# Flamingo block with experts: turned context and later weights laid out by the host, gate weights as one block of 16 columns

## The reference, cut to what matters

```python
x = x + tanh(g_xattn[0]) * xattn0(layernorm(x), ctx)   # 16 heads of 128, RMS-normed q and k, softmax
x = x + tanh(g_ffn[0])   * ffn0(layernorm(x))          # W, 8 LoRA experts of rank 16, top 2 by gate_w
x = x + tanh(g_xattn[1]) * xattn1(layernorm(x), ctx)   # Q'K / sqrt, sigmoid, V; Q, K, V are x, ctx, ctx
x = x + tanh(g_ffn[1])   * ffn1(layernorm(x))          # 8 experts of rank 64, the one with the largest logit
...
# ffn1
logits = xf @ Wg.T ; gate = argmax(softmax(logits)) ; h = (xf @ A.T) * one_hot(gate) ; y = h @ Bw * 4 * prob
```

## Time and profile before

| | us |
|---|---|
| median of 3 runs | 1327.33 |
| lowest and highest run | 1325.70, 1327.81 |
| span of the profiled execution | 1325.2 |
| own time of the profiled execution | not given beside its span |
| PE busy | 1310.4 |
| PE weight loads busy | 1156.5 |
| DVE busy | 765.3 |
| ACT busy | 737.2 |

### The profile page before, as it was taken

One profiled execution on the slowest core, in us unless ns is written; L12 is line 12 of the kernel. 1 busy time (PEld: TensorE's weight loads), 2 busy tenths in 40 slices (PEclk: granted clock), 3 DMA queues, 4 the chain that ended last, 5 costly groups with the idle time before them and its releaser, 6 DMA issues.

```text
span 1325.2 us, 26579 instructions
## 1 busy us (share of the span) xinstructions
PE 1310.4 (99%) x10358; PEld 1156.5 (87%) x10358; DVE 765.3 (58%) x2317; ACT 737.2 (56%) x2092; POOL 67.8 (5%) x112
## 2 busy tenths in 40 slices
PE   8999999999999999999999999999999999999998
PEld 8889899988999889988899888998889988898886
DVE  6744565646566465655556565564655645564585
ACT  4365666456456564656546554556646556556522
POOL 0000000010000000010000100001000010001010
PEclk9999999999999999999999999999999999999999
DMA  8311532133122321233212142122412122212101
GB/s 301 122 67 78 144 113 66 63 105 103 33 80 65 96 96 49 66 95 91 86 48 87 58 128 65 48 81 69 124 49 80 51 78 96 65 49 71 58 1 49
DMA packets 51451, 108.47 MB, mean 82 GB/s; under 512 B 8224, under 2 KB 32000, under 8 KB 50688
## 3 DMA queue, kind: packets, MB, share of 16 engines
q1 hardware_dynamic: 51328, 106.77, 25.0%
HBM read 89.98 MB, written 16.78 MB: 81 GB/s over the span
## 4 chain that ended last, share of the span: by engine, by line
PE 94%; DVE 4%; ACT 1%; issue 1%; POOL 0%; POOLq 0%; DVEq 0%
PE bank L114 64%; PE bank L1074 8%; PE bank L1084 5%; PE bank L1043 3%; PE bank L1184 2%; PE bank L1196 2%; PE bank L1063 2%; PE bank L1012 2%; PE bank L1033 1%; PE bank L1138 1%; PE bank L1226 1%; ACT logit L774 1%; PE bank L1050 0%; PE bank L1004 0%; PE bank L1348 0%
## 5 line engine op out<-in xcount | busy, mean ns | idle before, releaser
L774 ACT ACTIVATE logit<-logit,least 128x64 f32<-128x64 f32 x512 | 171.1, 338 | 179.7 <-DVE least L1625 179.7
L114 PE MATMUL bank<-sv,ct_hi 128*128 128x256 f32 x1024 | 195.8, 290 | 0.0
L114 PE MATMUL bank<-so,ao_hi 128*128 128x256 f32 x1008 | 193.9, 291 | 0.1
L114 PEld LDWEIGHTS bank<-sv,ct_hi 128*128 128x128 f32 x1024 | 158.2, 188 | 13.0 <-issue 10.7
L114 PEld LDWEIGHTS bank<-so,ao_hi 128*128 128x128 f32 x1008 | 153.4, 188 | 7.7 <-issue 7.6
L1074 PEld LDWEIGHTS bank<-pt,v_sb 128*128 128x128 f32 x1024 | 133.6, 191 | 11.1 <-ACT pt L782 0.3
L792 ACT ACTIVATE v_sb<-bank 128x512 f32<-128x512 f32 x128 | 76.2, 595 | 120.6 <-PE bank L114 120.6
L114 PE MATMUL bank<-sv,ct_lo 128*128 128x256 f32 x512 | 142.8, 279 | 0.0
L114 PE MATMUL bank<-so,ao_lo 128*128 128x256 f32 x504 | 140.5, 279 | 0.0
L1613 DVE SCALAR_TENSOR_TENSOR ao_lo<-bank,vecs,ao_hi 128x512 fp32r<-128x512 f32 x126 | 94.6, 751 | 76.9 <-ACT ao_hi L768 76.7
L1074 PE MATMUL bank<-pt,v_sb 128*128 128x128 f32 x1024 | 134.8, 274 | 0.1
(11 more groups left out here) (271 smaller groups left out, 2576.6 us busy)
## 6 DMA issues: line engine op xcount, KB each, us to landing
sv<-v_scratch SPq DMA_DIRECT2D x56, 512.0 KB, 3.4
so<-o_scratch SPq DMA_DIRECT2D x56, 512.0 KB, 3.3
xin<-in_x_dram SPq DMA_DIRECT2D x8, 512.0 KB, 5.1
cin<-in_ctx_dram SPq DMA_DIRECT2D x32, 128.0 KB, 4.9
xres<-in_x_dram SPq DMA_DIRECT2D x8, 512.0 KB, 4.7
c_scratch<-cs SPq DMA_DIRECT2D x8, 512.0 KB, 5.0
v_scratch<-sv SPq DMA_DIRECT2D x8, 512.0 KB, 2.7
o_scratch<-so SPq DMA_DIRECT2D x8, 512.0 KB, 2.6
```

Source lines behind the costliest of these rows:

```text
L114: last = pe.matmul(out, lhs[a], rhs[b], start=start and n == 0, stop=stop and n == 2, **kw)
L774: last = act.activation(logit[:, h % 2, t, :], logit[:, h % 2, t, :], ACT.Exp, scale=-1.0, bias=least[:, h % 2, t:t + 1], accum_out=rsum[: ...
```

## The change

The host hands over two more layouts of the context (`ctx_pairs` with two batches on the partitions, `ctx_turned` with features on the partitions), the five vectors as columns (`columns`), and all later weights turned and side by side in one tensor of 128 x 3104 (`later`). The kernel loads them as they are: one DMA for `cin`, one for `cs` (`load_turned`, step 3 of SP's queue; for group 0 ahead of k's weights), one for `ct`, one for `vecs`, one for `late_raw`. The transposes of context, later weights and vectors go, with the scratch tensor and its write. The transposes of x are gathered in two banks instead of four, at (7,e) and (8,c). The later weights are split from SBUF in five pieces. The expert gate's high and low parts stand as one block of 16 stationary columns, `gate_both`, which is multiplied with the high and with the low part of the tokens; DVE adds the two halves of the logits. So the product of both low parts, which was left out, is now in the sum.

```diff
+LATE = (0, DC * M0, DC * M0 + D, DC * M0 + D + DC * E1, DC * M0 + D + DC * E1 + DC * C1,
+        DC * M0 + D + DC * E1 + DC * C1 + CT1 * D)
-PREP_USES = 2 + 2 * 10
+PREP_USES = 1 + 2 * 10
...
-    TURN_AT = {(7, "e"): 0, (8, "b"): 1, (8, "c"): 2, (8, "d"): 3}
+    TURN_AT = {(7, "e"): 0, (8, "c"): 1}
...
-    LATE_AT = {(14, "c"): 0, (14, "e"): 1, (15, "a"): 2, (15, "b"): 3, (15, "c"): 4, (15, "d"): 5, (15, "e"): 6}
+    LATE_AT = {(14, "c"): 0, (14, "e"): 1, (15, "a"): 2, (15, "b"): 3, (15, "d"): 4}
...
-            for t in range(2):
-                for q in range(2):
-                    part = c_pairs[t, q]
-                    part = part[g:g + 1] if isinstance(g, int) else part[bass.ds(g, 1)]
-                    sp.dma_start(cin[t * SEQ:(t + 1) * SEQ, 2 * q:2 * q + 2, :],
-                                 part.rearrange("g b s d -> s (g b) d")).then_inc(cin_in.sem, 16)
+            sp.dma_start(cin[:, :, :], ctx_pairs[g]).then_inc(cin_in.sem, 16)
+
+        def load_turned(g):
+            split_lo.wait(sp, g - 1, 0)
+            if g > 0:
+                sp.wait_ge(gr_full.sem, gr_full.count(g - 1, NT - 1))
+            sp.dma_start(cs[:, :, :], ctx_turned[g]).then_inc(cs_in.sem, 16)
...
+            sp.dma_start(late_raw[:, :], later).then_inc(s_late, 16)
...
-                if h == 9 and not is_body(b, NG - 1):
-                    keep_context(b + 1)
+                if h == 3 and not is_body(b, NG - 1):
+                    load_turned(b + 1)
...
-        for j, v in enumerate((q_b, nq_s, nki_s, ki_b, vi_b)):
-            sp.dma_start(vrow[j * H:(j + 1) * H, :], v.rearrange("(h d) -> h d", h=H)).then_inc(s_vec, 16)
+        sp.dma_start(vecs[:, :], columns).then_inc(s_vec, 16)
...
         load_inputs(0)
+        load_turned(0)
...
-            act.activation(xs[:, :, t * P:(t + 1) * P], b[:, 0:D].rearrange("p (c n) -> p c n", c=DC), ACT.Copy)
-            act.activation(cs[:, :, t * P:(t + 1) * P],
-                           b[:, D:2 * D].rearrange("p (c n) -> p c n", c=DC), ACT.Copy).then_inc(tr_read.sem, 1)
+        def transposed(g, j):
+            act.wait_ge(tr_full.sem, tr_full.count(g, j))
+            act.activation(feature_major(xs, j), token_major(bank_of("tr", j, g)), ACT.Copy).then_inc(tr_read.sem, 1)
...
+            act.wait_ge(s_late, 16)
+            if u == 2:
+                act.activation(gate_both[:, :, 0:E1], gate_raw, ACT.Copy).then_inc(late_hi.sem, 1)
+                return
+            part = slice(LATE[u], LATE[u + 1])
+            act.activation(late_w[0][:, part], late_raw[:, part], ACT.Copy).then_inc(late_hi.sem, 1)
...
             for c in range(DC):
-                last = three(pe, dst[0:E1, :], [v[:, c, :] for v in g1t], [v[:, c, :] for v in x2t],
-                             start=c == 0, stop=c == DC - 1)
+                for n, v in enumerate(x2t):
+                    last = pe.matmul(dst[0:2 * E1, :], gate_both[:, c, :], v[:, c, :], start=c == 0 and n == 0,
+                                     stop=c == DC - 1 and n == 1)
...
-            if u == 0:
-                pe.wait_ge(s_late, 9 * 16)
-            for src, rows, at in late_uses[u][0]:
-                last = pe.transpose(dst[:, at:at + rows], src, ident[0:rows, 0:rows])
-            last.then_inc(late_full.sem, 1)
+        def transposes(b, j):
+            g = b + 1
+            if j == 0:
+                pe.wait_ge(xn_ready.sem, xn_ready.count(g, 0))
+                split_lo.wait(pe, g - 1, 1)
+            turned(g, "tr", j, xin, tr_full)
...
+            for c in range(DC):
+                pe.matmul(gate, gate_both[:, c, :], x2t[0][:, c, :], start=c == 0, stop=False, skip_group_check=True)
             pe.wait_ge(xt3_ready.sem, xt3_ready.count(LAST, 1))
+            for c in range(DC):
+                last = pe.matmul(gate, gate_both[:, c, :], x2t[1][:, c, :], start=False, stop=c == DC - 1,
+                                 skip_group_check=True)
...
-            dve.tensor_copy(coef[:, :, :], bank_of("lg", 0, s)[:, 0:NT * E1].rearrange("p (t e) -> p t e", t=NT)
-                            ).then_inc(lg1_read.sem, 1)
+            parts = bank_of("lg", 0, s)[:, 0:2 * NT * E1].rearrange("p (t n e) -> p t e n", t=NT, n=2)
+            dve.tensor_reduce(coef[:, :, :], parts, AXX, ALU.add).then_inc(lg1_read.sem, 1)
```

More of the change, by code:

```diff
@@ L115, in three, with two, third, layers @@
     return last
-def two(pe, out, lhs, rhs, start, low=0):
+def two(pe, out, lhs, rhs, start):
     for n in range(2):
[L121 to L130, removed]
+        pe.matmul(out, lhs[0], rhs[n], start=start and n == 0, stop=False, skip_group_check=True)
+def third(pe, out, lhs, rhs, stop):
+    return pe.matmul(out, lhs[1], rhs[0], start=False, stop=stop, skip_group_check=True)
+def layers(nc, stack, x, ctx, ctx_pairs, ctx_turned, g_xattn, g_ffn, q_w, ki_w, vi_w, o_w, o_b, columns,
+           b0, gate_b, later, out, v_dram, o_dram):
     x_t = x.rearrange("b s d -> (b s) d").rearrange("(g t p) d -> g p t d", g=NG, p=P)
     c_t = ctx.rearrange("b s d -> (b s) d").rearrange("(g t p) d -> g p t d", g=NG, p=P)
-    c_pairs = ctx.rearrange("(g q t b) s d -> t q g b s d", g=NG, q=2, t=2)
     out_t = out.rearrange("b s d -> (b s) d").rearrange("(g t p) d -> g p t d", g=NG, p=P)
@@ L395, in layers @@
     newest = [None] * 8
[L397 removed]
+    FIRST = [*((("tr", j, "N", tr_read), 6 + j) for j in range(2)),
              *((("gr", n, "N", gr_read), (6, 7, 0, 1, 4, 5, 6, 7)[n]) for n in range(2 * NT)),
@@ L841, in late_high @@
         def late_high(u):
-            act.wait_ge(late_full.sem, late_full.count(0, u))
-            for at, n, dst in late_uses[u][1]:
-                end = act.activation(dst[0], bank_of("late", u, 0)[:, at:at + n], ACT.Copy)
-            end.then_inc(late_hi.sem, 1)
+            act.wait_ge(s_late, 16)
[4 more added lines that the diff above has]
+            act.activation(late_w[0][:, part], late_raw[:, part], ACT.Copy).then_inc(late_hi.sem, 1)
         def choice_share(b, h, p):
@@ L1023, in take @@
             return bank
-        def transposes(b, t):
-            g, dst = b + 1, take("tr", t, b + 1)
-            if t == 0:
-                pe.wait_ge(xn_ready.sem, xn_ready.count(g, 0))
-                pe.wait_ge(cin_in.sem, cin_in.count(g, 63))
-                split_lo.wait(pe, g - 1, 1)
-            for n, src in enumerate((xin, cin)):
-                for c in range(DC):
-                    last = pe.transpose(dst[:, (2 * n + c) * P:(2 * n + c + 1) * P], src[:, t, c * P:(c + 1) * P],
-                                        ident[:, :])
-            last.then_inc(tr_full.sem, 1)
         def gram_products(b, t):
             g = b + 1
-            pe.wait_ge(tr_read.sem, tr_read.count(g, t))
+            pe.wait_ge(tr_read.sem, tr_read.count(g, t // 2))
+            if t == 0:
+                pe.wait_ge(cs_in.sem, cs_in.count(g, 15))
             for n, src in enumerate((xs, cs)):
@@ L1381, in last_choice @@
         def last_choice():
-            rows, gate = take("h", 0, LAST), take("gt", 0, LAST)[0:E1, :]
+            rows, gate = take("h", 0, LAST), take("gt", 0, LAST)[0:2 * E1, :]
             row_parts = [([v[:, c, 0:P] for v in x2t], [v[:, c, :] for v in a1t]) for c in range(DC)]
-            gate_parts = [([v[:, c, :] for v in g1t], [v[:, c, :] for v in x2t]) for c in range(DC)]
             pe.wait_ge(xt3_hi_ready.sem, xt3_hi_ready.count(LAST, 0))
@@ L1389, in last_choice @@
             pe.wait_ge(xt3_hi_ready.sem, xt3_hi_ready.count(LAST, 1))
-            for c, (lhs, rhs) in enumerate(gate_parts):
-                two(pe, gate, lhs, rhs, start=c == 0, low=1)
+            for c in range(DC):
+                pe.matmul(gate, gate_both[:, c, :], x2t[0][:, c, :], start=c == 0, stop=False, skip_group_check=True)
             pe.wait_ge(xt3_ready.sem, xt3_ready.count(LAST, 1))
-            for c, (lhs, rhs) in enumerate(gate_parts):
-                last = third(pe, gate, lhs, rhs, stop=c == DC - 1, low=1)
+            for c in range(DC):
+                last = pe.matmul(gate, gate_both[:, c, :], x2t[1][:, c, :], start=False, stop=c == DC - 1,
+                                 skip_group_check=True)
             last.then_inc(gt_full.sem, 1)
@@ L1450, in _ @@
         warm(8)
-        pe.wait_ge(s_vec, 80)
-        pe.transpose(banks[TURN_BANKS][:, 0:5 * H], vrow[:, :], ident[0:5 * H, 0:5 * H]).then_inc(s_prep, 1)
         pe.wait_ge(s_chain, BSQ_READY)
```

165 lines of the change are left out of this document (62 added, 103 removed).

## The result

The kernel after takes 1311.28 us (median of 4 runs, 1310.84 to 1313.52), the kernel before 1327.57 beside it (4 runs, 1325.70 to 1327.89): a ratio of 0.9883, 95% interval 0.9869 to 0.9897, or 16.3 us less. The forecast was 1313.1 us, or 14.2 less. The profiled execution took 1310.84 us, with a span of 1309.0.

The account below looks back on a forecast made before the run. PE's queue was taken as the bound, its work priced by start-to-start spacing. 6.2 + 3.3 + 3.4 + 1.3 = 14.2 us off span 1325.2 gave 1311.0, plus 2.1 to the median: 1313.1 us, range 1308.5 to 1320.

Parts of the forecast that it names:

- the restarts: PE's restart after a removed transpose section; if it goes too, the upper bound is 1.0 us a group.
- Context transposes: Groups 1 to 7 each lose 8 of 16 PE transposes at 0.11 us: 6.2 us less.
- Gate block: Expert gate: four products for six per group, 0.46 us less in six dense bodies and the tail, none in group 6: 3.3.
- Later weights: Body 0, steps 14 and 15: 28 transposes and a 1.51 us stall go, 4.7 gross, 1.3 given back: 3.4 net.
- The start: Start: ones product 1.0 us earlier, k weight copies 0.35 earlier; 1.3 us less, bounds 0 and 2.5.
- the ones product can go when the first eight warming products end: Start: with one load filling `vecs`, the ones product goes at 5.51 instead of 6.53, 1.0 us.
- could end it sooner: Start: an earlier start might end the slow transpose spacing sooner, or fall wholly on it and take 0.9 us back.
- The moved load: `load_turned` at step 3 of SP's queue, replacing the `cs` write at step 9, delays nothing: cost 0.
- rival (c): Every group: the read of `cs` delays weight fetches, PE stands 2.4 us in each of seven bodies: 1330 us, chance 0.03.
- (a): Bodies: PE isn't alone, ACT and DVE answers absorb part of the gain: 7.3 us less, 1320 us, chance 0.10.
- (b): Removed PE work counts by duration, 272 ns a transpose and 394 a product: 30.9 us less, 1296 us, chance 0.03.
- (d): Removed PE work was not on the path and the start's DMA eats its gain: 1326 us, chance 0.04.

Follow-up runs that it names:

- gate_only: Kernel before with only the gate's 16-column block, two products per chunk and the sum on DVE; 1324.05 us, ratio 0.9977.
- before_full: Kernel before with two more warm-up products between the turn of the vectors and the ones product; median 1325.73 us.
- start_gap: Kernel after with six unread DVE instructions delaying the ones product, so that PE idles ahead of it; 1312.93 us.
- turned_twice: Kernel after with each group's x turned twice in groups 1 to 7, 8 transposes more per group; 1318.45 us.

## Why the prediction was right, and where it was off

The mechanism held: PE's queue is the limit, and what leaves it is worth its spacing. Of the 2.1 us by which the gain was larger than forecast, 1.3 are the start, in part chance, and 0.7 the restarts; the gate's 0.2 less and the later weights' 0.2 more cancel.

- **Context transposes, 6.2 us forecast.** Right in mechanism and price: 0.109 each, 6.1 us. With one restart a group (0.1, not isolated) about 6.9. I had put 1.0 us a group as the upper bound for just that, and it came out at 0.98.
- **Gate block, 3.3.** 0.45 in each of six bodies and 0.4 in the tail make 3.1; the kernel with this part alone measured 3.0. Group 6 gave nothing, as said: after its gate PE now waits 0.49 us for `prob` (at 1237.79), where it had 0.04 before (at 1253.53).
- **Later weights, 3.4 net.** 4.6 us of body 0 less the context's 1.0 leave 3.6. The gross size was right (28 transposes cost 3.0 when put back, and the 1.51 stall is gone with the bank use it waited for), and so was the sum given back, 1.3 forecast and 0.70 + 0.57 found. Its parts were not: I named q, `ct_lo` and `xt_lo`. The `ct_lo` wait was there, mostly from another cause (a split of `o_w` ahead of it in DVE's queue), and the second wait was for `k_sb`.
- **The start, 1.3: the term that was mis-sized.** The profiles differ by 2.6. The failed step is "the ones product can go when the first eight warming products end ... That is 1.0 us". It went 1.2 us earlier (5.30), but it is not what the first k product waits for. Of the 2.6 us, 0.66 belong to k's stage (29.25 less 28.59; I had 0.35). The other 1.95 are the profiled kernel before, whose full clock came at 10.23, after about nine slow transposes, against the profiled kernel after, whose full clock came at 6.64 and whose load landed early. Against `gate_only`, whose unchanged start had the fast spacing, the gain is 1.39, and with a late landing (10.96) nothing of the whole 1.4 is left. My clause that the earlier start "could end it sooner" was the right worry, with 0.9 us as its size; filling the gap was worth 1.0. The prediction took a granted clock of 1.00 for the slow stretch from the earlier trace rows, but that window starts at 10.00, where the stretch ends, and ahead of 10.23 the record has no entry: so the slow spacing fits the lower level, and no reading of 1.00 speaks against it.
- **The moved load, 0.** PE never waits for `cs`. The fetches of output weights land in 3.3 us as before, so rival (c) has nothing to stand on.
- **Rivals.** (a), PE isn't alone, falls with the 0.45 and 0.87 us per body; (b), durations count, falls with the same rows; (d) with the result.

The terms as measured, 6.9 + 3.1 + 3.6 + 2.6, make the 16.2 of the span. The 2.1 us that I carried from span to median fit for the kernel after too (1311.28 - 1309.0 = 2.3), though an execution's own time is just 1.8 above its span (1310.84 and 1309.0). The rest is the distance of the profiled execution from the median; that it came out nearly alike in both kernels is luck.

## What to carry to other kernels

Where windows repeat and one engine's queue is dense, cost an edit by that engine's start-to-start spacing, and add about 0.1 us for a section of another kind that goes, unless it stands beside one of its own kind. Where a removed piece had stood between a producer and its consumer, read the producer's queue too: what gives the gain back may be an instruction that merely stands ahead of the one waited for. And at a start, take two or three profiles of the same kernel before pricing it, since a landing or a clock that varies by more than the edit moves all that follows.

## What the runs showed of the hardware

- At the start PE runs f32 passes of 128 columns 0.213 us apart, later 0.109, about half. I read them as the spacings of the levels of 1.2 and 2.4 GHz: the clock records begin with the full clock where the spacing changes (10.23 us in the kernel before, 6.64 in the kernel after). In nine profiles without PE idle time from 1.76 us to the ones product, the full clock was there by 7.73; in the four in which PE fell idle before it had come, it came at 10.23 to 11.26.
- Four of the fourteen profiled executions (`gate_only`, `before_full`, `start_gap`, `turned_twice`) have, ahead of their last microseconds, a stretch of 3.4 us with the granted clock at half; the runs don't show why. A window of `turned_twice` catches it:

```profile
11.00:15.50 4.50, 4.15 (x15) 3.19 (x13) 2.50 (x6) 1.71 (x1) 0.00 (x0) 0.62 1.04 427
```

Its first k product comes 30.27 us after the block of `q_w` (10.20 to 40.47) and not 28.59: the stretch cost this execution 1.7 us. `start_gap` has its own near the end, 0.7 us by the tail behind the last scores (74.15 and not 73.47).
- In one execution, keeping other loads off the queues did not bring a 1 MB load home sooner (10.87 against 9.50 us, issued at the same time, with starts of 9.47 to 10.96 in kernels that don't hold them back).
